# A third sum moved behind a softmax's multiplication, and VectorE steps given to ScalarE, in a four-layer fused kernel

## What is computed

```python
x = x + L0_conv(_ln_c(x))     # deformable convolution: 8 groups of 32 channels, 9 points each, bilinear sampling
t = t + L0_ffn(_ln_t(t))      # mixture of experts: 8 experts, 128 -> 512 -> 128, top 1, capacity 640
x = x + L1_conv(_ln_c(x))     # neighbourhood attention: 8 heads, 7x7 windows, relative bias
t = t + L1_ffn(_ln_t(t))      # a second mixture of experts
```

## Time and profile before

| what | value |
| --- | --- |
| median of 3 runs | 2625.39 us (2617.28 to 2628.91) |
| the profiled execution | 2640.72 us |
| its span, from first to last instruction | 2638.7 us |
| PE busy | 2204.0 us, 84% |
| DVE busy | 2139.2 us, 81% |
| ACT busy | 1242.1 us, 47% |
| POOL busy | 1668.6 us, 63% |
| mean granted TensorE clock | 0.917 of full |

### The profile page before, as it was taken

One profiled execution on the slowest core, in us unless ns is written; L12 is line 12 of the kernel. 1 busy time (PEld: TensorE's weight loads), 2 busy tenths in 40 slices (PEclk: granted clock), 3 DMA queues, 4 the chain that ended last, 5 costly groups with the idle time before them and its releaser, 6 DMA issues.

```text
span 2638.7 us, 55380 instructions
## 1 busy us (share of the span) xinstructions
PE 2204.0 (84%) x17088; PEld 2070.2 (78%) x17088; DVE 2139.2 (81%) x4147; ACT 1242.1 (47%) x3704; POOL 1668.6 (63%) x1797
## 2 busy tenths in 40 slices
PE   1677888888889888888888888888888988988787
PEld 1467788787888787788878788888888888888777
DVE  4589898889888889888888888888988889888632
ACT  1223354454444455544445454444555545455555
POOL 3577777777666766666676666667676666677000
PEclk6778799999999999999999999999999999999898
DMA  8422222222211222221122222122111111121000
GB/s 187 132 62 59 63 61 58 65 65 63 59 53 51 66 59 60 62 61 53 52 65 60 59 59 61 51 54 65 56 57 56 54 55 55 48 59 57 15 23 4
DMA packets 220276, 158.65 MB, mean 60 GB/s; under 512 B 149994, under 2 KB 187516, under 8 KB 220124
## 3 DMA queue, kind: packets, MB, share of 16 engines
q0 software_dynamic: 55296, 113.36, 14.9%
q1 hardware_dynamic: 163804, 43.50, 7.5%
q10 hardware_dynamic: 1024, 0.26, 0.1%
HBM read 138.67 MB, written 18.04 MB: 59 GB/s over the span
## 4 chain that ended last, share of the span: by engine, by line
PE 47%; DVE 28%; issue 15%; ACT 4%; SPq 2%; DMA 2%; DVEq 2%; ACTq 0%
PE N L1357 11%; PE Z L1450 10%; PE Y L1460 8%; DVE made L916 8%; DVE got L998 4%; PE N L1366 3%; PE N L1530 2%; PE N L1512 2%; PE N L1522 2%; DVE summed L1001 2%; DMA xt_m<-cold_T 2%; SPq L659 1%; PE N L1504 1%; ACT L1232 1%; DVE prob L1133 1%
## 5 line engine op out<-in xcount | busy, mean ns | idle before, releaser
L775 POOL DMA_INDIRECT got<-patches,ranks x1728 | 1653.7, 957 | 739.1 <-issue 501.8
L1357 PE MATMUL N<-ident,made 128*128 128x128 f32 x4608 | 610.5, 287 | 189.5 <-DVE made L916 185.5
L916 DVE TENSOR_TENSOR made<-held,tent 128x1024 f32<-128x1024 f32 x576 | 678.9, 1217 | 100.2 <-issue 71.2
L1259 ACT ACTIVATE hid<-Z,b 128x128 f32<-128x128 f32 x2048 | 580.9, 368 | 350.7 <-PE Z L1450 348.5
L1357 PEld LDWEIGHTS N<-ident,made 128*128 128x128 f32 x4608 | 541.3, 149 | 231.8 <-DVE made L916 186.2
L1450 PE MATMUL Z<-xt_m,w 128*128 128x128 f32 x4096 | 586.2, 292 | 25.5 <-DMA xt_m<-cold_T 25.0
L1460 PE MATMUL Y<-w,hid 128*128 128x128 f32 x4096 | 575.1, 285 | 34.8 <-ACT hid L1259 34.8
L1450 PEld LDWEIGHTS Z<-xt_m,w 128*128 128x128 f32 x4096 | 546.5, 207 | 39.0 <-issue 15.6
L1460 PEld LDWEIGHTS Y<-w,hid 128*128 128x128 f32 x4096 | 523.0, 200 | 49.9 <-ACT hid L1259 41.5
L1001 DVE TENSOR_REDUCE summed<-got 128x32 f32<-128x1152 f32 x192 | 411.3, 2142 | 6.6
L998 DVE TENSOR_TENSOR got<-got,held 128x1152 f32<-128x1152 f32 x192 | 258.6, 1347 | 3.8
(11 more groups left out here) (204 smaller groups left out, 2215.6 us busy)
## 6 DMA issues: line engine op xcount, KB each, us to landing
got<-patches,ranks POOLq DMA_INDIRECT x1728
vwin<-vpad SPq DMA_DIRECT2D x320, 40.0 KB
patches<-arena SPq DMA_DIRECT2D x92, 96.0 KB
w<-in_L_ffn_w SPq DMA_DIRECT2D x2, 2048.0 KB
patches<-got SPq DMA_DIRECT2D x38, 96.0 KB, 3.0
vpad<-vt SPq DMA_DIRECT2D x128, 16.0 KB
out<-X SPq DMA_DIRECT2D x32, 64.0 KB, 1.9
xt_m<-cold_T ACTq DMA_DIRECT2D x64, 4.0 KB
```

The lines of the kernel that those rows point to most:

```text
L775: pool.indirect_dma_start(out=got[:, q, j * PATCH:(j + 1) * PATCH], out_offset=None, in_=table, in_offset=bass.IndirectOffsetOnAxis(ap=ran ...
L916: v.tensor_tensor(made[:, k % MADE, :].rearrange("p (y x) -> p y x", y=H), across.unsqueeze(2).to_broadcast([P, H, W]), tent[:, 0, k, :].u ...
L1259: ins = a.activation(hid[:, e % 2, c, :], Z[e % 2][:, c * P:(c + 1) * P], ACT.Relu, bias=b1[n][:, e * FC + c:e * FC + c + 1])
L1357: ins = pe.matmul(N[c // 4][:, (c % 4) * P:(c % 4 + 1) * P], made[:, k % MADE, c * P:(c + 1) * P], ident[:, :], start=(k % K == 0 and c % ...
```

## The change

Five edits, all inside the engines' functions:

1. The third group's step is split: its multiplication stays in front of the softmax's `weights`, its sum comes behind.
2. The norms of the tiles for values and places are done by ScalarE as scale and bias (`rs_p` and a new `nm_p` = -mean * rs, one more VectorE instruction in each `measure`).
3. The biases of queries and keys are added by ScalarE; the queries' bias is scaled beforehand in the setup. VectorE's addition for the values now waits for the keys, and so does `spread`.
4. The second half of the attention's output is copied by ScalarE behind the first.
5. Three additions of epsilon a slot are gone; the root takes epsilon from a small tile as its bias operand.

```diff
                     if e == 0:
                         if e1:
                             close(u1, 1, i - 4)
-                        conv(2, i)
+                        conv(2, i, "weigh")
                         if att:
                             attend("weights", i - 3)
+                        conv(2, i, "reduce")
...
@@ VectorE
-                if part == "norm":
-                    xt = X[:, bass.ds(t, 1), :].rearrange("p o d -> p (o d)")
-                    v.wait_ge(*val_t.done("xT", t - 1))
-                    v.tensor_scalar(xn_p, xt, mv_p[:, bass.ds(t, 1), 0:1].rearrange("p o a -> p (o a)"),
-                                    rs_p[:, bass.ds(t, 1)], ALU.subtract, ALU.mult).then_inc(*s("xn"))
...
+                v.scalar_tensor_tensor(out=nm_p[:, t0:t1], in0=mv_p[:, t0:t1, 0:1].rearrange("p t a -> p (t a)"),
+                                       scalar=-1.0, in1=rs_p[:, t0:t1], op0=ALU.mult, op1=ALU.mult)\
+                    .then_inc(measured, 1)
...
+            for n, value in enumerate((1e-5, 1e-6)):
+                v.memset(eps[:, n:n + 1], value).then_inc(eps_set, 1)
...
+            v.tensor_scalar(bq[:, 0:1], bq[:, 0:1], HD ** -0.5, None, ALU.mult).then_inc(setup, 1)
+            v.wait_ge(setup, 8 + NH)
...
-                    v.wait_ge(*d("aggr", t))
-                    v.tensor_scalar(sd_m[:, 0:1], mv_m[:, 1:2], 1e-5, None, ALU.add).then_inc(*s("eps"))
...
-                    v.wait_ge(*d("aggr", t))
-                    v.tensor_scalar(sd_q[:, 0:1], mv_q[:, 1:2], 1e-6, None, ALU.add).then_inc(*s("eps"))
...
                 if part == "project":
-                    r = t % QRING
-                    v.wait_ge(*qkv_t.done("qkv", t))
-
-                    v.tensor_scalar(QT[:, bass.ds(r, 1), :, :].rearrange("p o j (a c) -> p (o a) j c", a=BLK),
-                                    M[:, 128:256].rearrange("p (a j c) -> p a j c", a=BLK, j=NB),
-                                    bq[:, 0:1], HD ** -0.5, ALU.add, ALU.mult).then_inc(*s("q"))
-                    kr = (t // TB) % RING * PH + (t % TB) * TILE_ROWS + HALO
-                    v.tensor_scalar(KT[:, bass.ds(kr, TILE_ROWS), HALO:HALO + W],
-                                    M[:, 256:384].rearrange("p (a w) -> p a w", a=TILE_ROWS),
-                                    bq[:, 1:2], None, ALU.add).then_inc(*s("k"))
-
+                    v.wait_ge(*qkv_s.done("k", t))
                     v.wait_ge(*v_out.through(t - 1))
                     v.tensor_tensor(vt[:, :], M[:, 384:512], bv[:, :], ALU.add).then_inc(*s("v"))
...
                 if part == "spread":
+                    v.wait_ge(*qkv_s.done("k", t))
                     v.wait_ge(*att_t.done("s1", t - 1))
...
-                if part == "values":
-                    v.wait_ge(*att_t.done("o", t))
-                    v.tensor_copy(OT_of[:, :, 1, :], N[1][:, :].rearrange("p (g w) -> p g w", g=NH * BLK)).then_inc(*s("o1"))
...
@@ ScalarE
+                if part == "norm":
+                    xt = X[:, bass.ds(t, 1), :].rearrange("p o d -> p (o d)")
+                    a.wait_ge(*val_t.done("xT", t - 1))
+                    a.activation(xn_p, xt, ACT.Identity, scale=rs_p[:, bass.ds(t, 1)], bias=nm_p[:, bass.ds(t, 1)])\
+                        .then_inc(*val_s.step("xn"))
...
-                    a.wait_ge(*route_v[n].done("eps", t))
-                    a.activation(sd_m[:, 1:2], sd_m[:, 0:1], ACT.Sqrt).then_inc(*s("std"))
+                    a.wait_ge(*route_v[n].done("aggr", t))
+                    a.activation(sd_m[:, 1:2], mv_m[:, 1:2], ACT.Sqrt, bias=eps[:, 0:1]).then_inc(*s("std"))
...
+                if part == "project":
+                    r = t % QRING
+                    kr = (t // TB) % RING * PH + (t % TB) * TILE_ROWS + HALO
+                    a.wait_ge(*qkv_t.done("qkv", t))
+
+                    a.activation(QT[:, bass.ds(r, 1), :, :].rearrange("p o j (a c) -> p (o a) j c", a=BLK),
+                                 M[:, 128:256].rearrange("p (a j c) -> p a j c", a=BLK, j=NB),
+                                 ACT.Identity, scale=HD ** -0.5, bias=bq[:, 0:1]).then_inc(*s("q"))
+                    a.activation(KT[:, bass.ds(kr, TILE_ROWS), HALO:HALO + W],
+                                 M[:, 256:384].rearrange("p (a w) -> p a w", a=TILE_ROWS),
+                                 ACT.Identity, bias=bq[:, 1:2]).then_inc(*s("k"))
...
                     a.wait_ge(*att_t.done("o", t))
-                    a.activation(OT_of[:, :, 0, :], N[0][:, :].rearrange("p (g w) -> p g w", g=NH * BLK), ACT.Copy)\
-                        .then_inc(*s("o0"))
+                    for k in range(2):
+                        a.activation(OT_of[:, :, k, :], N[k][:, :].rearrange("p (g w) -> p g w", g=NH * BLK), ACT.Copy)\
+                            .then_inc(*s(f"o{k}"))
...
@@ TensorE
-                    pe.wait_ge(*qkv_v.done("k", after))
+                    pe.wait_ge(*qkv_s.done("k", after))
...
-                    pe.wait_ge(*att_v.done("o1", t))
-                    pe.wait_ge(*att_s.done("o0", t))
+                    pe.wait_ge(*att_s.done("o1", t))
```

More of the change, by code:

```diff
@@ L180, in build @@
         st_p, mv_p = sb("st_p", [P, NT, 6]), sb("mv_p", [P, NT, 2])
-        rs_p = sb("rs_p", [P, NT])
+        rs_p, nm_p = sb("rs_p", [P, NT]), sb("nm_p", [P, NT])
+        eps = sb("eps", [P, 2])
         got = sb("got", [P, NQ, QJ * PATCH])
@@ L271, in build @@
         setup = sem("setup")
+        eps_set = sem("eps_set")
         shifted_t, shifted_s = sem("shifted_t"), sem("shifted_s")
         masked = [Landed(sem(f"masked{n}")) for n in range(2)]
-        val_v = Steps(sem("val_v"), "xn vals dense")
-        val_s = Steps(sem("val_s"), "xT")
+        val_v = Steps(sem("val_v"), "vals dense")
+        val_s = Steps(sem("val_s"), "xn xT")
         val_t = Steps(sem("val_t"), "xT vals")
-        place_v = Steps(sem("place_v"), "xn offs e1 sig off pos clamp spot spotw near "
+        place_v = Steps(sem("place_v"), "offs e1 sig off pos clamp spot spotw near "
                         "floor frac frac0 in0 in1 w0 w1 wy wq flc lin rank")
-        place_s = Steps(sem("place_s"), "xT exp")
+        place_s = Steps(sem("place_s"), "xn xT exp")
         place_t = Steps(sem("place_t"), "xT offs")
@@ L295, in build @@
         conv_s = Steps(sem("conv_s"), "T")
-        route_v = [Steps(sem(f"route{n}_v"), "stats aggr eps rstd xn lg max neg eqd first hot rsum pos taken "
+        route_v = [Steps(sem(f"route{n}_v"), "stats aggr rstd xn lg max neg eqd first hot rsum pos taken "
                          "kept in gate") for n in range(2)]
@@ L302, in build @@
         exp_t = Steps(sem("exp_t"), "z0 z1 y0 z2 y1 z3 y2 z4 y3 z5 y4 z6 y5 z7 y6 y7")
[L303 to L304 removed]
+        qkv_v = Steps(sem("qkv_v"), "stats aggr rstd xn v")
+        qkv_s = Steps(sem("qkv_s"), "std xT q k")
         qkv_t = Steps(sem("qkv_t"), "xT qkv")
[L306 to L307 removed]
+        att_v = Steps(sem("att_v"), "qbd s0 s1 max neg rsum norm add")
+        att_s = Steps(sem("att_s"), "exp0 exp1 p0 p1 o0 o1")
         att_t = Steps(sem("att_t"), "s0 s1 p0 p1 o proj")
@@ L807, in places @@
                 d, s = place_v.done, place_v.step
[L808 to L812, removed]
                 if part == "offsets":
@@ L981, in _ @@
             v.wait_ge(setup, 7 + NH)
+            v.tensor_scalar(bq[:, 0:1], bq[:, 0:1], HD ** -0.5, None, ALU.mult).then_inc(setup, 1)
+            v.wait_ge(setup, 8 + NH)
             def conv(part, t, placed=None):
                 d, s = conv_v.done, conv_v.step
-                if isinstance(part, int):
+                if isinstance(part, int) and placed != "reduce":
                     q = part
@@ L999, in conv @@
                         .then_inc(*s(f"m{q}"))
+                if isinstance(part, int) and placed != "weigh":
+                    q = part
                     v.wait_ge(*d(f"m{q}", t))
@@ L1169, in places @@
                 s = place_s.step
+                if part == "norm":
+                    xt = X[:, bass.ds(t, 1), :].rearrange("p o d -> p (o d)")
+                    a.wait_ge(measured, 2 * LEAD + 4 + (2 * (NT - LEAD) + 4 if not isinstance(t, int) or t > 0 else 0))
+                    a.wait_ge(*place_t.done("xT", t - 1))
+                    a.activation(xn_o, xt, ACT.Identity, scale=rs_p[:, bass.ds(t, 1)], bias=nm_p[:, bass.ds(t, 1)])\
+                        .then_inc(*s("xn"))
                 if part == "turn":
@@ L1211, in _ @@
                 places(part, 0)
-            measure(LEAD, NT, 2 * LEAD + 3)
+            measure(LEAD, NT, 2 * LEAD + 4)
             for part in PLACES:
@@ L1215, in _ @@
             dense("tents", 0)
+            a.wait_ge(eps_set, 2)
             a.wait_ge(const_in, CONSTS)
@@ L1282, in qkv @@
                 if part == "norm":
-                    a.wait_ge(*qkv_v.done("eps", t))
-                    a.activation(sd_q[:, 1:2], sd_q[:, 0:1], ACT.Sqrt).then_inc(*s("std"))
+                    a.wait_ge(*qkv_v.done("aggr", t))
```

(7 more changed lines are left out.)

2 lines of the change are left out of this document (1 added, 1 removed).

## The result

The median fell from 2627.15 us (4 runs, 2617.28 to 2641.98) to 2563.18 us (4 runs, 2558.26 to 2566.76): a ratio of 0.974, 95% interval 0.970 to 0.978. Forecast were 2593 us and a range of 2565 to 2634. The time lies 2 us under the range, and the gain of 64 us is twice the 32 that were forecast. The experiments show that it is not the gain that the working describes: it comes from a stall of VectorE's instruction stream that the change removed by the way.

A forecast was written before the change was run, and what follows sets the result against it. No single engine bounds the kernel; the order of work inside a slot does. First-loop slots -33 us, last eight +3 after edge costs, setup and tail 2 at most: sum -32, from 2625.39 to 2593, range 2565 to 2634.

The forecast's parts named there:

- the loop edge: VectorE's idle between loop turns: first loop's 3.69 us stall stays, second loop begins to stall, +19 us.
- the loops fit: Second rival, chance 0.10: loop body shortens below what is held, first loop's turns stop stalling, -49 us, second's +17 unpaid: 2527.
- Low clock: TensorE's reduced clock, costing 2.74 us in a mean first-loop slot; the change was to make it rarer and cheaper.
- Low clock stays: Rival, chance 0.27: TensorE's idle time only moves, so the clock still falls; a slot gains 1.05 us: 2617.
- D: Stretch from softmax multiplication's end to attention's addition into X: 9.65 us at full clock to become 10.7, VectorE leading.
- C: Stretch from query, key and value projection to softmax multiplication's end, VectorE leading: 13.75 us to become 13.1.
- Queries and keys: Their biases move to ScalarE at the projection: 0.54 us leave VectorE, values come 0.25 later, bounds -0.2 and +0.8.
- Slower: ScalarE's queue: Rival, chance 0.09: late keys and exponentials hold VectorE up after the projection, a slot gets 1.05 us longer: 2645.
- B: Stretch of TensorE's sums and projections until the next qkv, TensorE leading: 13.80 us at full clock, nothing gained there.
- E+A: Stretch from attention's addition to the first tent map after routing's normalization, VectorE leading: 37.80 us to become 37.45.
- Epsilon's -0.35: Three additions of 0.154 us a slot leave VectorE before the roots: -0.35 us per slot, bounds 0 and -0.55.
- the slots' 33 + 15: Forecast gains from shorter slots: 33 us over the first loop's 18, 15 over the last eight before edge costs.

The follow-up runs named there:

- before_moved24: The kernel before with 24 idle memsets of an unused tile added in VectorE's setup, slots' work untouched: 2551.5 us, ratio 0.968 to the kernel before.
- the longer body: The changed kernel with 16 unused semaphore increments in VectorE's loop body (267 instructions): 2571.9 us; with eight idle memsets in setup too, 2625.2 us.

## Why the prediction was wrong

**The step that failed is the loop edge.** It took the stall of the first loop as staying and gave the second one as well, +19. Neither came: 0.42 for 3.69 at the first, and the second stayed held. The mechanism was named rightly (parts of 8 KB, their number set by the place), but the length was measured in operations that do work, 127 to 119, and called 6% shorter. What counts is all instructions between two branches: 271 to 251. With parts of 128, up to 257 instructions never touch a fourth; 271 can, in 14 of 128 places (271 - 257), and 251 in none. The place, which no row shows, had become irrelevant. The second rival, "the loops fit", had this right and got 0.10. The rule that was cited gave the same: with the pages of 256 instructions of the Trainium skill (Runtime: NRT & Kernel Launch, Instruction fetch mechanics), a body of 251 touches two at most. The runs don't tell its pages of 256 from four parts of 128.

**Low clock.** The forecast let its price fall from 2.74 to 0.85 us per first-loop slot. It is 74.00 - 72.11 = 1.9 (72.11 is the slot of four stretches above; none ran wholly at full clock). And what it fell by came with the edge: in before_moved24, without any of the five edits, it is 1314.50 / 18 - 71.60 = 1.43. "Low clock stays" was nearer. Ahead of D, 0.97 and 2.48 were to become 1.2 and 1.6; they became 1.47 and 1.55, and the runs show both to matter: the split took 25 us from the wait for the weights and saved 31 to 34 us of time; queries and keys added 14 us to the wait for the ReLU and cost 53, C's 11 among them.

**Queries and keys.** Forecast: 0.25 later for the values, bounds -0.2 and 0.8; measured 1.30 - 0.77 = 0.53, inside the bounds. C became 13.50 instead of 13.1. The mis-sized term is what hangs on it: 53 us for the move. "Slower: ScalarE's queue" described it, exponentials pushed by late keys included, at 0.09; its place was right, but in the time the edge and the split covered it. A side remark was wrong without a cost: the scores do wait for this slot's keys, but these are done at 1125.64 and the scores begin at 1126.10.

**What held.** D at full clock 10.62 (10.7 forecast), B 13.71 (13.80), VectorE's idle 1.18 (1.1), the wait for the weights 1.55 (1.6), the norms worth nothing, the copy 0.6. E+A was to be 37.45; with the edge's 3.27 (3.69 - 0.42) added, 34.28 is 37.55. Epsilon's -0.35 is not to be seen when it alone is undone: VectorE's longer wait for the dearer root takes it back. The prediction saw that price (0.28 of the gain) and set it aside. The Trainium skill (ScalarE: Activation LUTs, What ACT_TABLE_LOAD costs) gives about 93 ns for a pointer operand; the 92 ns here agree.

**The sum again**, from the ratios: the edge 0.968; the split on top 0.956; epsilon, norms and copy 0.954, no more than their intervals; queries and keys on ScalarE 0.974. Beside the sum of the prediction: the edge gains 85 us where 19 were to be paid, 104 better. Queries and keys cost 53 where their 0.25 made 26 x 0.25 = 7, 46 worse. The other edits bring (0.968 - 0.954) x 2637 = 37 where the slots' 33 + 15 and those 7 made 55, 18 worse. That the time lies only 2 us under the range is luck: these errors cancel in great part. The second rival's 2527 foresaw the held loop, at 49 of its 85 us, and lay too low by the other two errors.

What stays open: why the same waits leave the clock up in one slot and not in the next. In the 18 first-loop slots of the change the wait for the weights is 1.54 or 1.55 us and that for the ReLU 1.46 to 1.62, and D is 10.62 or 12.16.

## What to carry to other kernels

Before costing a change to a looped kernel, count all instructions between the branches on each engine and look at the instruction queue's packets per turn: 24 idle instructions ahead of the loop were worth 85 us here, and eight cost 53 in the longer body, as much as the largest effect of the five edits. Then compare edits at the same edge; else a gain from the place is booked to the edit. When a step goes to another engine, follow what stands behind its result there and here: ordering the consumer that the lead needs first, and the moved work after it, turned a loss of 53 us into a gain of 26 here (0.954 to 0.944).

## What the runs showed of the hardware

The edge of a loop body of 267 or 271 instructions on VectorE takes 0.3 us or 2.8 to 4.1 by where it lies; eight instructions of shift decide (267: held, then not). In these runs TensorE's clock decided what a saved microsecond was worth: 1.0 us of VectorE's work taken from D gave nothing (2488.7 against 2489.7), since low clock came back in D or behind it, while 0.9 us a slot taken from the wait ahead of D, with VectorE's sum moved into D, gave 31 to 34 us over the kernel, more than the 25 us of waiting. A root of 128x1 takes 203 ns with a constant bias and 295 with one from a tile.
